# Attention rows in two PSUM banks, scores in 32x32 tiles, and a new order of all calls, in a fused attention and FP4 feed-forward layer

## The chip, the cores and the metric

The kernel runs on one core of one Trainium2 chip. The metric is device time in microseconds, the median of several executions of the whole program.

## What is computed

One layer over 2048 tokens of width 128: retention (linear attention with a decay for each of 8 heads, 16 wide for queries and keys, 32 for values) with an output gate, a residual and a layer norm; then a feed-forward part of width 352 whose operands are all rounded to FP4 in blocks of 16, a residual and a second layer norm. In the reference (cut):

```python
q, k, v = (split_heads(hidden_states @ W) for W in (Wq, Wk, Wv)); q, k = rope(q), rope(k)
scores = jnp.einsum('bhqd,bhkd,hqk->bhqk', q * DQK ** (-0.5), k, decay)
o = jnp.einsum('bhqk,bhkd->bhqd', scores, v)
o = o * jax.lax.rsqrt(jnp.mean(o * o, axis=-1, keepdims=True) + EPS) * g_norm_w
x = layernorm(x + (o.reshape(b, l, VDIM) * silu(hidden_states @ Wg)) @ Wo)
h = silu(fp4_linear(x, w_gate)) * fp4_linear(x, w_up)    # fp4_linear rounds both operands
x = layernorm(x + fp4_linear(h, w_down))
```

## The kernel before

The tokens are 16 chunks `c` of 128, each of two halves `a` of 64. There is no loop over chunks in the program: each engine has one list, written out, of calls such as `scores(5)`, and works through it in order. A call first waits on semaphores for what it reads and, on TensorE (`occupy`, `free`), until the last user of each of its PSUM banks has been read out; then it issues its instructions. So the order of the five lists decides what stands behind what. SyncE's list holds only loads and stores, and ACT's weight loads stand ahead of its list.

One chunk goes through these steps. TensorE projects (`project_qk`, `project_vg`); VectorE multiplies by the rotation tables (`rotate`), POOL adds (`rotate_add`), TensorE transposes (`transpose_qk`) and ACT copies out (`q_even`, `q_odd`, `k_transposed`). `scores` (L330) multiplies keys by queries within each half; VectorE masks them (`mask_scores`, L727). The state `S` of each half comes from `state_product` (L341) and VectorE's `next_state` (L738). The rows of the attention are accumulated in PSUM, transposed (32 features of a head by 64 tokens): `from_state` (L355) starts them with state times query, `values` (L365) adds value times masked score. ACT copies them out (`copy_oT`), `transpose_o` (L372, L373) turns them to tokens by 256 features, ACT squares (`squares`), VectorE gates (`gated`, L748) and sums (`mean_square`), POOL takes the power -1/2 (`rms_rstd`) and multiplies (`gated_output`). Then `transpose_y`, `copy_yT`, `out_projection` (L386 to L388), `ln1_squares`, `ln1_norm`; the rounding of x (`x_amax` to `x_grid_` on VectorE, `x_value` on POOL), `transpose_xq`, `gate` (L421), `up` (L427), `h_product`, the rounding of h likewise (`h_amax`, `h_inv`, `h_ratio_`, `h_plus_`, `h_grid_`, `h_value`), `transpose_h` (L433), `down` (L441), `ln2_sum` and the second norm. At the start VectorE also rounds the two weight tensors (`weights_amax(0)` to `weights_value(1)`); TensorE transposes them (`transpose_gate_up_weights`, `transpose_down_weights`) before it can run `gate(0)`.

All products are in f32. A call of `mm` shows as two weight loads and two matmuls in the trace, a transposition as one of each.

PSUM has 8 banks of 512 f32 columns. Scores of heads 2j and 2j+1 lie in bank j of 0 to 3, one row of tiles for 32 query or key features (row group j of TensorE) by 64 keys. The attention rows of half `a` and heads 4h to 4h+3 lie in bank 2h+a: all four banks 0 to 3. Of the same four, bank 0 also serves `transpose_qk`, bank 1 `transpose_o` (until `gated` has read it), bank 2 `transpose_xq`, bank 3 `transpose_h`. Up to four chunks' buffers exist in SBUF (`c % D`, D = 4), and six of `h_ratio`.

Of the kernel before, what the change touches and what calls it, by code (L numbers as in the profile page):

```python
# [74 lines left out]
def seq_postln_kernel(nc, x, xt, wqk, wvg, wo_g, w_gate_up, w_down, tab, cst, out):  # L75
# [4 lines left out]
    with ExitStack() as ctx:  # L80
# [3 lines left out]
        def sem(name):  # L84
# [76 lines left out]
        BANKS = {"sc": (0, 1, 2, 3), "oT": (0, 1, 2, 3), "o": (1,), "yT": (7,), "qk": (4,), "qkT": (0,),  # L161
                 "vg": (6,), "att": (5,), "xqT": (2,), "gate": (4,), "hT": (3,), "up": (7,),
# [4 lines left out]
        oT_ps = ps[:, 0:4, 0:CH]  # L167
        oT_bank = lambda half, a: ps[:, BANKS["oT"][2 * half + a], 0:CH]
# [12 lines left out]
        wg_T_ps, wu_T_ps = ps[:, 3, 0:I], ps[:, 2, 0:I]  # L181
# [63 lines left out]
        def _(pe_engine):  # L245
# [76 lines left out]
            def scores(c):  # L322
# [22 lines left out]
            def from_state(c):  # L345
# [44 lines left out]
            def transpose_gate_up_weights():  # L390
                pe.wait_ge(c_ident, 1)
                pe.wait_ge(wq_v[0], 1)
                occupy("wgu", (3, 2))
# [50 lines left out]
            warm_up(4); project_qk(0); project_vg(0); transpose_qk(0); project_qk(1); state_product(0); scores(0)  # L444
# [495 lines left out]
```

## Time and profile before

| what | value |
|---|---|
| median of 3 executions | 133.14 us (133.12 to 134.86) |
| the profiled execution | 132.9 us, of which the span from first to last instruction is 131.2 us |
| granted TensorE clock, mean | 0.992 of full speed |
| busy share: TensorE matmuls, VectorE, ACT, POOL | 91%, 84%, 68%, 67% |

Busy time is the union of the instructions' durations. A matmul's duration holds the time in which its results drain, and the next one starts before that; an instruction of VectorE or ACT likewise overlaps the next by about 0.1 us. So a pace is read from one start to the next, not from the durations alone.

### The profile page before, as it was taken

How to read it: one execution, taken by the hardware profiler on the slowest of the kernel's cores; microseconds unless marked ns; L12 is line 12 of the kernel's file. 1: busy time of each engine (PE TensorE's matmuls, PEld its weight loads, DVE VectorE, ACT ScalarE, POOL GpSimd, SP SyncE). 2: the span in 40 equal slices, each digit the busy share in tenths (PEclk: the TensorE clock that was granted, in tenths of full speed). 3: DMA queues.
4: the chain of work that ended last, by engine and by line, in shares of the span. 5: the costliest groups of instructions: out<-in, count | busy, mean ns of one | idle time of the engine just before them, and what ended most of it. 6: DMA issues, size and time to landing. Idle time of an engine off the chain costs nothing.

```text
span 131.2 us, 5084 instructions
## 1 busy us (share of the span) xinstructions
PE 119.2 (91%) x2040; PEld 82.7 (63%) x2040; DVE 110.0 (84%) x329; ACT 88.8 (68%) x311; POOL 87.7 (67%) x124
## 2 busy tenths in 40 slices
PE   4859699989999999999999999899999999999860
PEld 4425257766667676766675576567696788887650
DVE  1249999689589999999999998899999999999810
ACT  3143847557674776839576858778696878898882
POOL 5202726577687849784783869476949797996781
PEclk9999999999999999999999999999999999999996
DMA  3899991000000000000000000000000000011222
GB/s 104 256 273 392 425 440 45 5 5 5 0 5 0 5 0 5 0 7 0 5 2 5 0 5 2 5 0 5 0 5 0 25 2 0 20 40 30 58 80 80
DMA packets 4791, 7.68 MB, mean 59 GB/s; under 512 B 800, under 2 KB 3872, under 8 KB 4512
## 3 DMA queue, kind: packets, MB, share of 16 engines
q1 hardware_dynamic: 3744, 6.60, 14.3%
q10 hardware_dynamic: 1024, 0.76, 1.8%
q8 instruction: 16, 0.26, 0.9%
q14 instruction: 7, 0.06, 0.2%
HBM read 6.31 MB, written 1.05 MB: 56 GB/s over the span
## 4 chain that ended last, share of the span: by engine, by line
PE 66%; DVE 16%; DMA 6%; issue 4%; ACT 3%; POOL 2%; SPq 1%; POOLq 0%; DVEq 0%
PE ps L313 7%; PE ps L441 7%; DMA tabs_sb<-rope_tables 6%; PE ps L421 6%; PE ps L427 6%; PE ps L330 5%; PE ps L307 4%; PE ps L355 4%; PE ps L365 4%; DVE probs L727 3%; PE ps L433 3%; PE ps L386 3%; PE ps L341 3%; PE ps L388 2%; PE ps L387 2%
## 5 line engine op out<-in xcount | busy, mean ns | idle before, releaser
L859 POOL TENSOR_TENSOR rstd_h<-ms,minus_half 128x8 f32<-128x8 f32 x16 | 26.8, 1672 | 6.9 <-DVE ms L743 6.8
L313 PE MATMUL ps<-w_vg,xT_sb 128*128 128x512 f32 x32 | 17.4, 625 | 1.5 <-DVE S L738 1.1
L854 POOL TENSOR_TENSOR qk<-rope 128x256 f32<-128x256 f32 x16 | 11.7, 729 | 9.7 <-DVE rope L721 9.7
L878 POOL TENSOR_TENSOR xq<-x_ratio,xs 128x128 f32<-128x128 f32 x16 | 7.8, 489 | 11.9 <-DVE x_ratio L656 11.9
L441 PE MATMUL ps<-wd_T,hT 128*128 128x128 f32 x96 | 14.1, 283 | 1.3 <-DVE r L757 0.7
L721 DVE TENSOR_TENSOR rope<-ps,tabs_sb 128x512 f32<-128x512 f32 x16 | 11.0, 687 | 4.6 <-DMA tabs_sb<-rope_tables 3.3
L870 POOL TENSOR_TENSOR rstd<-veps,minus_half 128x1 f32<-128x1 f32 x16 | 9.3, 579 | 7.7 <-DVE veps L752 7.7
L886 POOL TENSOR_TENSOR hq<-h_ratio,hs 128x352 f32<-128x352 f32 x16 | 13.0, 815 | 1.7 <-DVE h_ratio L656 1.4
L441 PEld LDWEIGHTS ps<-wd_T,hT 128*128 128x128 f32 x96 | 12.1, 191 | 3.1 <-ACT hT L483 1.5
L727 DVE TENSOR_TENSOR probs<-ps,causal 128x512 f32<-128x512 f32 x16 | 11.0, 690 | 2.8 <-PE ps L330 2.4
L421 PE MATMUL ps<-wgu_T,xqT 128*128 128x352 f32 x32 | 13.3, 496 | 0.0
L483 ACT ACTIVATE oT<-ps 128x256 f32<-128x256 f32 x16 | 6.1, 382 | 9.9 <-PE ps L365 9.8
L427 PE MATMUL ps<-wgu_T,xqT 128*128 128x352 f32 x32 | 12.2, 464 | 0.0
L307 PE MATMUL ps<-w_qk,xT_sb 128*128 128x256 f32 x32 | 10.8, 421 | 1.0 <-DMA xT_sb<-x_transposed 1.0
L864 POOL TENSOR_TENSOR y<-gate_o,rstd_h 128x256 f32<-128x256 f32 x16 | 10.4, 651 | 0.5
L484 ACT ACTIVATE q_eo<-ps,consts 128x128 f32<-128x128 f32 x32 | 10.7, 376 | 0.0
L738 DVE SCALAR_TENSOR_TENSOR S<-S,consts,ps 128x64 f32<-128x64 f32 x31 | 8.3, 269 | 2.6 <-PE ps L341 2.2
L874 POOL TENSOR_TENSOR rstd<-veps,minus_half 128x1 f32<-128x1 f32 x16 | 9.1, 579 | 1.5 <-ACT r_sq L580 1.5
L483 ACT ACTIVATE v_sb<-ps 128x256 f32<-128x256 f32 x16 | 6.3, 391 | 5.0 <-PE ps L313 5.0
L561 ACT ACTIVATE silu_h<-ps 128x352 f32<-128x352 f32 x16 | 7.4, 463 | 2.8 <-PE ps L421 2.5
L501 ACT ACTIVATE h_magic<-h_ratio 128x352 bf16<-128x352 f32 x16 | 7.9, 496 | 1.5 <-DVE h_ratio L647 1.4
L483 ACT ACTIVATE hT<-ps 128x384 f32<-128x384 f32 x16 | 7.8, 487 | 1.6 <-PE ps L433 1.6
(110 smaller groups left out, 340.1 us busy)
## 6 DMA issues: line engine op xcount, KB each, us to landing
tabs_sb<-rope_tables SPq DMA_DIRECT2D x1, 2048.0 KB, 12.0
tabs_sb<-rope_tables SPq DMA_DIRECT2D x1, 1280.0 KB, 8.1
out<-x SPq DMA_DIRECT2D x16, 64.0 KB, 1.5
tabs_sb<-rope_tables SPq DMA_DIRECT2D x1, 512.0 KB, 4.6
xT_sb<-x_transposed SPq DMA_DIRECT2D x1, 512.0 KB, 7.6
xT_sb<-x_transposed SPq DMA_DIRECT2D x1, 320.0 KB, 5.5
tabs_sb<-rope_tables SPq DMA_DIRECT2D x1, 256.0 KB, 3.6
w_vg<-in_w_vg ACTq DMA_DIRECT2D x1, 256.0 KB, 3.9
```

The costliest lines, as they stand in the source:

```text
L307: mm(qk_ps, xT(c), w_qk[:], start=True, stop=True).then_inc(qk_pe, 1)
L313: mm(vg_ps, xT(c), w_vg[:], start=True, stop=True).then_inc(vg_pe, 1)
L421: mm(gate_ps, xqT[:, c % D, :], wgu_T[:, 0:I], start=True, stop=True).then_inc(gate_pe, 1)
L427: mm(up_ps, xqT[:, c % D, :], wgu_T[:, I:2 * I], start=True, stop=True).then_inc(up_pe, 1)
L441: last = mm(down_ps, hT[:, c % D, t, :], wd_T[:, t, :], start=t == 0, stop=t == 2)
L483: copy = lambda o, i: nc.scalar.activation(o, i, ACT.Copy)
L484: scaled = lambda o, i, by: nc.scalar.activation(o, i, ACT.Identity, scale=by)
L721: vec.tensor_tensor(rope[:, c % D, :, :], qk_ps.unsqueeze(1).to_broadcast([128, 2, 256]), tabs(c).rearrange("p (t n) -> p t n", t=2), ALU. ...
L727: vec.tensor_tensor(probs[:, c % D, :, :].rearrange("p (j e) q -> p j e q", e=2), all_sc_ps.rearrange("p j (e q) -> p j e q", e=2), causal ...
L854: gp.tensor_tensor(g16(qk[:, c % D, :]), g16(rope[:, c % D, 0, :]), g16(rope[:, c % D, 1, :])[:, :, ::-1, :], ALU.add).then_inc(qk_p, 1)
L859: gp.tensor_tensor(rstd_h[:, c, :], ms[:, c, :], minus_half[:], ALU.pow).then_inc(rms_p, 1)
L886: gp.tensor_tensor(hq[:, c % D, 0:I].rearrange("p (n k) -> p n k", k=BLK), h_ratio[:, c % 6, :].rearrange("p (n k) -> p n k", k=BLK), hs[: ...
```

## The change

- The attention rows lie in two banks: half `a` in bank 1+a, with the even heads in columns 0 to 63 and the odd in 64 to 127 (`oT_ps(a)`). Heads 2j and 2j+1 stand in the 32 partitions of slot `(j + 2a) % 4`: in the second half the upper and lower 64 partitions are swapped. `from_state` and `values` run over e (even, odd) outside.
- `copy_oT` becomes three ACT instructions: the first half whole (128 partitions by 128), the second half in two pieces of 64 partitions by 128 that undo the swap.
- `transpose_o` thus gives the features in the order (e, j, d); `squares` and `gated` read PSUM through views that put them back. `o` moves to bank 2, `xqT` to bank 1, the transposed weights to banks 1 and 3.
- `scores` runs over four groups of 32 keys in place of two of 64: 16 calls of `mm` for 8.
- `h_ratio_(c)` waits for POOL's `h_value(c - 6)`, the last reader of its buffer.
- The lists of TensorE, ACT, VectorE and POOL are ordered anew. The sets of calls are the same, SyncE's list and all DMAs are as before.

```diff
-        BANKS = {"sc": (0, 1, 2, 3), "oT": (0, 1, 2, 3), "o": (1,), "yT": (7,), "qk": (4,), "qkT": (0,),
-                 "vg": (6,), "att": (5,), "xqT": (2,), "gate": (4,), "hT": (3,), "up": (7,),
+        BANKS = {"sc": (0, 1, 2, 3), "oT": (1, 2), "o": (2,), "yT": (7,), "qk": (4,), "qkT": (0,),
+                 "vg": (6,), "att": (5,), "xqT": (1,), "gate": (4,), "hT": (3,), "up": (7,),
...
-        oT_ps = ps[:, 0:4, 0:CH]
-        oT_bank = lambda half, a: ps[:, BANKS["oT"][2 * half + a], 0:CH]
+        oT_ps = lambda a: ps[:, BANKS["oT"][a], 0:C].rearrange("p (e q) -> p e q", q=CH)
+        oT_slot = lambda j, a: 32 * ((j + 2 * a) % NP)
...
-                for a in range(2):
+                for k in range(4):
                     for j in range(NP):
-                        rows, keys = slice(32 * j, 32 * j + 32), slice(CH * a, CH * a + CH)
+                        rows, keys = slice(32 * j, 32 * j + 32), slice(32 * k, 32 * k + 32)
                         last = mm(sc_ps(j)[keys, :], kT[rows, c % D, keys],
-                                  q_eo[rows, c % D, a, :, :].rearrange("p e q -> p (e q)"), start=True, stop=True)
+                                  q_eo[rows, c % D, k // 2, :, :].rearrange("p e q -> p (e q)"), start=True, stop=True)
...
-                for a in range(2):
-                    for n in range(NH):
-                        j, e, slot32 = n // 2, n % 2, n % 4
-                        rows = slice(32 * j, 32 * j + 32)
-                        mm(oT_bank(n // 4, a)[32 * slot32:32 * slot32 + 32, :], S[rows, (2 * c + a) % 8, e * DV:(e + 1) * DV],
-                           q_eo[rows, c % D, a, e, :], start=True, stop=False)
+                for e in range(2):
+                    for a in range(2):
+                        for j in range(NP):
+                            rows, slot = slice(32 * j, 32 * j + 32), oT_slot(j, a)
+                            mm(oT_ps(a)[slot:slot + 32, e, :], S[rows, (2 * c + a) % 8, e * DV:(e + 1) * DV],
+                               q_eo[rows, c % D, a, e, :], start=e == 0, stop=False)
...
-                for n in range(NH):
-                    slot32 = n % 4
-                    for a in range(2):
-                        keys = slice(CH * a, CH * a + CH)
-                        last = mm(oT_bank(n // 4, a)[32 * slot32:32 * slot32 + 32, :],
-                                  v_sb[keys, c % D, n * DV:(n + 1) * DV], probs[keys, c % D, n, :], start=False, stop=True)
+                for e in range(2):
+                    for j in range(NP):
+                        for a in range(2):
+                            n, keys, slot = 2 * j + e, slice(CH * a, CH * a + CH), oT_slot(j, a)
+                            last = mm(oT_ps(a)[slot:slot + 32, e, :], v_sb[keys, c % D, n * DV:(n + 1) * DV],
+                                      probs[keys, c % D, n, :], start=False, stop=e == 1)
...
-                copy(oT[:, c % D, :, :, :].rearrange("p h a q -> p (h a) q"), oT_ps).then_inc(oT_act, 1)
+                copy(oT[:, c % D, :, 0, :], oT_ps(0))
+                copy(oT[0:64, c % D, :, 1, :], oT_ps(1)[64:128])
+                copy(oT[64:128, c % D, :, 1, :], oT_ps(1)[0:64]).then_inc(oT_act, 1)
...
-                nc.scalar.activation(o_sq[:, c % D, :, 0:DV], o_ps.rearrange("p (h d) -> p h d", d=DV), ACT.Square,
+                nc.scalar.activation(o_sq[:, c % D, :, 0:DV].rearrange("p (j e) d -> p j e d", e=2),
+                                     o_ps.rearrange("p (e j d) -> p j e d", e=2, d=DV), ACT.Square,
...
-                vec.tensor_tensor(gate_o[:, c % D, :], o_ps, silu_g[:, c % D, :], ALU.mult).then_inc(gate_v, 1)
+                vec.tensor_tensor(jed(gate_o[:, c % D, :]), o_ps.rearrange("p (e j d) -> p j e d", e=2, d=DV),
+                                  jed(silu_g[:, c % D, :]), ALU.mult).then_inc(gate_v, 1)
...
-            def h_ratio_(c): quant_ratio(h(c), sh(c), blocks(h_ratio[:, c % 6, :]), hquant_v, c)
+            def h_ratio_(c):
+                if c >= 6:
+                    dve.wait_ge(hq_p, c - 5)
+                quant_ratio(h(c), sh(c), blocks(h_ratio[:, c % 6, :]), hquant_v, c)
```

The lists, as far as the text below speaks of them. TensorE, the start and two later places:

```diff
-            warm_up(4); project_qk(0); project_vg(0); transpose_qk(0); project_qk(1); state_product(0); scores(0)
-            project_vg(1); from_state(0); values(0); state_product(1); project_qk(2); transpose_qk(1); transpose_o(0)
...
-            transpose_o(1); transpose_qk(2); transpose_gate_up_weights(); state_product(2); transpose_down_weights()
...
-            state_product(3); values(2); project_qk(5); transpose_o(2); transpose_qk(3); out_projection(1)
-            state_product(4); scores(3); project_qk(6); from_state(3); values(3); project_qk(7); transpose_qk(4)
-            transpose_o(3); transpose_y(2); transpose_xq(0); project_vg(5); gate(0); scores(4); out_projection(2)
...
-            from_state(4); state_product(5); values(4); project_qk(8); transpose_o(4); transpose_qk(5); transpose_y(3)
-            project_vg(6); transpose_xq(1); up(0); scores(5); out_projection(3); from_state(5); state_product(6)
-            values(5); gate(1); transpose_o(5); transpose_qk(6); transpose_y(4); project_vg(7); project_qk(9)
-            transpose_xq(2); up(1); scores(6); out_projection(4); from_state(6); state_product(7); values(6); gate(2)
+            warm_up(4); project_qk(0); project_vg(0); transpose_qk(0); state_product(0); scores(0); project_qk(1)
+            project_vg(1); from_state(0); values(0); state_product(1); transpose_qk(1); project_qk(2); transpose_o(0)
...
+            project_qk(4); transpose_y(0); transpose_o(1); transpose_gate_up_weights(); transpose_down_weights()
...
+            state_product(3); transpose_qk(3); project_qk(5); transpose_o(2); out_projection(1); state_product(4)
+            scores(3); project_qk(6); from_state(3); values(3); transpose_qk(4); project_qk(7); transpose_y(2)
+            transpose_o(3); transpose_xq(0); project_vg(5); scores(4); gate(0); out_projection(2); from_state(4)
...
+            transpose_xq(1); up(0); scores(5); out_projection(3); gate(1); from_state(5); state_product(6); values(5)
+            transpose_qk(6); project_qk(9); transpose_y(4); transpose_o(5); project_vg(7); transpose_xq(2); up(1)
+            scores(6); out_projection(4); from_state(6); state_product(7); values(6); gate(2); transpose_qk(7)
```

ACT, VectorE and POOL, the start:

```diff
-            copy_v(0); silu_g_(0); q_even(0); q_odd(0); k_transposed(0); silu_g_(1); copy_v(1); copy_oT(0); squares(0)
+            silu_g_(0); k_transposed(0); copy_v(0); q_odd(0); q_even(0); weights_magic(0); copy_v(1); silu_g_(1)
+            copy_oT(0); k_transposed(1); squares(0); q_odd(1); q_even(1); copy_v(2); silu_g_(2); weights_magic(1)
...
-            rotate(0); weights_amax(0); next_state(0, 0); next_state(0, 1); rotate(1); mask_scores(0); weights_inv(0)
-            weights_amax(1); weights_ratio(0); next_state(1, 0); rotate(2); next_state(1, 1); mean_square(0)
-            weights_inv(1); gated(0); weights_ratio(1); weights_plus(0); mask_scores(1); weights_grid(0)
+            rotate(0); weights_amax(0); weights_inv(0); next_state(0, 0); weights_ratio(0); next_state(0, 1)
+            rotate(1); mask_scores(0); scale_wo(); weights_plus(0); weights_amax(1); next_state(1, 0); weights_inv(1)
+            next_state(1, 1); rotate(2); gated(0); mean_square(0); weights_ratio(1); mask_scores(1); weights_grid(0)
...
-            rotate_add(5); rms_rstd(3); gated_output(3); ln1_rstd(2); x_value(1); rotate_add(6); rms_rstd(4)
+            rotate_add(5); rotate_add(6); rms_rstd(3); rotate_add(7); gated_output(3); ln1_rstd(2); x_value(1)
```

## Rows read from the trace of the kernel before

**Rows 1.** The page, part 1: busy time, share of the span, instructions of each engine.

```profile
PE 119.2 (91%) x2040; PEld 82.7 (63%) x2040; DVE 110.0 (84%) x329; ACT 88.8 (68%) x311; POOL 87.7 (67%) x124
```

**Rows 2.** The page, part 4: shares of the chain that ended last.

```profile
PE 66%; DVE 16%; DMA 6%; issue 4%; ACT 3%; POOL 2%; SPq 1%; POOLq 0%; DVEq 0%
```

**Rows 3.** Table by stretch: busy time of each engine (instructions), then granted clock, DMA.

```profile
10.00:20.00 10.00, 8.57 (x184) 4.74 (x185) 9.93 (x24) 5.73 (x17) 3.78 (x4) 1.00 1.02 413
20.00:40.00 20.00, 19.55 (x430) 13.20 (x428) 16.25 (x47) 12.95 (x47) 14.37 (x18) 1.00 0.02 7
40.00:100.00 60.00, 59.09 (x1175) 40.44 (x1153) 57.03 (x178) 42.94 (x154) 43.43 (x56) 1.00 0.01 3
100.00:125.00 25.00, 23.85 (x219) 19.10 (x218) 23.24 (x70) 20.90 (x77) 20.88 (x31) 1.00 0.08 23
```

**Rows 4.** Timeline of TensorE, 44 to 51 us: start, length, instruction, count.

```profile
44.39 0.47 PE L330 MATMUL ps<-q_eo,kT 32*64 32x128 f32 x16
...
46.76 0.86 PE L421 MATMUL ps<-wgu_T,xqT 128*128 128x352 f32 x2
47.45 0.27 PE L372 MATMUL ps<-ident,oT 128*128 128x128 f32 x1
...
48.11 1.02 PE L313 MATMUL ps<-w_vg,xT_sb 128*128 128x512 f32 x2
48.97 0.59 PE L307 MATMUL ps<-w_qk,xT_sb 128*128 128x256 f32 x2
...
50.20 0.63 PE L330 MATMUL ps<-q_eo,kT 32*64 32x128 f32 x16
```

**Rows 5.** Timeline of VectorE, 4 to 24 us; in brackets idle time and its end.

```profile
9.24 0.60 DVE L738 SCALAR_TENSOR_TENSOR S<-S,consts,ps 128x64 f32<-128x64 f32 x2 [1.48 <-PE ps L341]
...
11.05 0.33 DVE L673 TENSOR_SCALAR wr_small<-wr_small 128x44 f32<-128x44 f32 x1
...
11.80 0.51 DVE L639 TENSOR_REDUCE wr_small<-wd_nat 128x22 f32<-128x352 f32 x1
12.22 0.88 DVE L647 SCALAR_TENSOR_TENSOR wr_ratio<-wgu_nat,wr_small 128x704 f32<-128x704 f32 x1
...
16.56 0.68 DVE L727 TENSOR_TENSOR probs<-ps,causal 128x512 f32<-128x512 f32 x1
```

**Rows 6.** Timeline of TensorE, 5 to 33 us: two blocks.

```profile
8.05 0.70 PE L307 MATMUL ps<-w_qk,xT_sb 128*128 128x256 f32 x2 [1.01 <-DMA xT_sb<-x_transposed]
...
24.54 0.45 PE L355 MATMUL ps<-q_eo,S 32*32 32x64 f32 x32
```

**Rows 7.** Groups of instructions: count, busy us, mean ns; idle time before them.

```profile
L483 ACT ACTIVATE oT<-ps 128x256 f32<-128x256 f32 x16 | 6.1, 382 | 9.9 <-PE ps L365 9.8
...
L483 ACT ACTIVATE xqT<-ps 128x128 f32<-128x128 f32 x16 | 4.5, 280 | 1.4 <-PE ps L415 1.2
...
L727 DVE TENSOR_TENSOR probs<-ps,causal 128x512 f32<-128x512 f32 x16 | 11.0, 690 | 2.8 <-PE ps L330 2.4
```

**Rows 8.** Waits: who for whom, total us, times, longest.

```profile
PEld ps L372 <- ACT oT L483: 2.9, 10, 0.4
...
PEld ps L330 <- ACT q_eo L484: 3.5, 6, 1.2
```

**Rows 9.** Timeline of TensorE, 5 to 33 us: the same block twice.

```profile
11.96 0.44 PE L341 MATMUL ps<-v_sb,qk 64*32 64x64 f32 x16
...
20.62 0.34 PE L341 MATMUL ps<-v_sb,qk 64*32 64x64 f32 x16
```

**Rows 10.** Timeline, 26 to 33 us: transposed rows and their gating, chunk 3.

```profile
30.91 0.27 PE L372 MATMUL ps<-ident,oT 128*128 128x128 f32 x1
...
32.20 0.37 DVE L748 TENSOR_TENSOR gate_o<-ps,silu_g 128x256 f32<-128x256 f32 x1
```

**Rows 11.** Timeline, 96 to 110 us: POOL's `h_value(6)` and VectorE's `h_ratio_(12)`.

```profile
103.01 0.89 POOL L886 TENSOR_TENSOR hq<-h_ratio,hs 128x352 f32<-128x352 f32 x1 [0.38 <-PE ps L433]
...
109.01 0.52 DVE L647 SCALAR_TENSOR_TENSOR h_ratio<-h_blocks,hs 128x352 f32<-128x352 f32 x1
```

More of the change, by code:

```diff
@@ L458, in _ @@
-            transpose_qk(8); transpose_y(6); project_vg(9); project_qk(11); transpose_xq(4); up(3); scores(8)
-            out_projection(6); from_state(8); state_product(9); values(8); gate(4); transpose_qk(9); transpose_o(8)
-            transpose_y(7); project_vg(10); project_qk(12); transpose_xq(5); up(4); scores(9); out_projection(7)
-            from_state(9); state_product(10); values(9); gate(5); transpose_o(9); transpose_qk(10); transpose_y(8)
-            project_vg(11); project_qk(13); up(5); transpose_xq(6); out_projection(8); scores(10); gate(6)
@@ L463, in _ @@
-            from_state(10); state_product(11); values(10); project_qk(14); transpose_o(10); transpose_qk(11)
-            project_vg(12); transpose_xq(7); transpose_y(9); scores(11); up(6); out_projection(9); from_state(11)
-            state_product(12); values(11); gate(7); transpose_qk(12); transpose_o(11); transpose_y(10); project_vg(13)
-            project_qk(15); up(7); transpose_xq(8); out_projection(10); scores(12); gate(8); from_state(12)
-            values(12); state_product(13); transpose_o(12); transpose_qk(13); transpose_y(11); project_vg(14)
@@ new lines, in _ @@
+            transpose_xq(1); up(0); scores(5); out_projection(3); gate(1); from_state(5); state_product(6); values(5)
+            transpose_qk(6); project_qk(9); transpose_y(4); transpose_o(5); project_vg(7); transpose_xq(2); up(1)
+            scores(6); out_projection(4); from_state(6); state_product(7); values(6); gate(2); transpose_qk(7)
+            transpose_o(6); transpose_y(5); project_vg(8); project_qk(10); transpose_xq(3); up(2); scores(7)
+            out_projection(5); from_state(7); state_product(8); values(7); gate(3); transpose_qk(8); transpose_o(7)
@@ new lines, in _ @@
+            transpose_y(6); project_vg(9); project_qk(11); transpose_xq(4); up(3); scores(8); out_projection(6)
+            gate(4); from_state(8); state_product(9); values(8); transpose_qk(9); project_qk(12); transpose_y(7)
+            transpose_o(8); project_vg(10); transpose_xq(5); up(4); scores(9); out_projection(7); from_state(9)
+            state_product(10); values(9); transpose_qk(10); gate(5); transpose_o(9); transpose_y(8); project_vg(11)
+            project_qk(13); transpose_xq(6); out_projection(8); scores(10); gate(6); up(5); from_state(10); values(10)
@@ new lines, in _ @@
+            state_product(11); transpose_qk(11); project_qk(14); transpose_o(10); transpose_y(9); project_vg(12)
+            transpose_xq(7); out_projection(9); scores(11); up(6); from_state(11); values(11); state_product(12)
+            transpose_qk(12); gate(7); transpose_o(11); transpose_y(10); project_vg(13); project_qk(15)
+            transpose_xq(8); up(7); scores(12); out_projection(10); from_state(12); state_product(13); values(12)
+            gate(8); transpose_qk(13); transpose_o(12); transpose_y(11); project_vg(14); up(8); transpose_xq(9)
@@ new lines, in _ @@
+            out_projection(11); scores(13); gate(9); from_state(13); state_product(14); values(13); transpose_qk(14)
+            transpose_h(0); transpose_y(12); transpose_o(13); project_vg(15); up(9); transpose_xq(10)
+            out_projection(12); scores(14); gate(10); from_state(14); state_product(15); values(14); transpose_y(13)
+            transpose_qk(15); transpose_o(14); transpose_h(1); up(10); out_projection(13); transpose_xq(11); down(0)
+            scores(15); gate(11); up(11); from_state(15); values(15); transpose_y(14); transpose_h(2); down(1)
@@ L829, in _ @@
+            h_grid_(13); h_plus_(14); ln2_sum(10); h_grid_(14); h_product(15); h_amax(15); ln2_sum(11); h_inv(15)
+            h_ratio_(15); ln2_sum(12); h_plus_(15); h_grid_(15); ln2_sum(13); ln2_sum(14); ln2_sum(15)
         @block.gpsimd
```

203 lines of the change are left out of this document (97 added, 106 removed).

## Prediction

> **What bounds the kernel now.** I read the busy shares first: TensorE 91%, VectorE 84%, ACT 68%, POOL 67% [rows 1]. Two engines are nearly full, so the next view is the chain that ended last: 66% of the span on TensorE and 16% on VectorE [rows 2]. Then the table by stretch tells where VectorE idles: 0.07 us between 10 and 20 us, 3.75 us between 20 and 40, 2.97 us between 40 and 100, 1.76 us between 100 and 125 [rows 3]. That is 8.5 us in 115, and since the change takes no work from VectorE, no order gains more than this and what lies ahead of 10 us. Last the timelines. From one `scores` to the next (44.39 to 50.20 us) TensorE has 5.81 us of work end to end: the six transpositions from 47.45 to 48.11 follow each other at 0.11 us, `project_vg` takes 0.86 [rows 4]. In the middle, then, TensorE sets the pace with VectorE just behind; in the start (10 to 20 us) it is VectorE, with the rounding of the weights; at the end the backlog of h on VectorE.
>
> The profiled execution took 132.9 us: a span of 131.2 and 1.7 around it. I make the sum against 132.9 and add 0.2 us at the end, by which the median of 133.14 lies above it.
>
> **The start: -1.2 us.** VectorE idles 1.48 us until 9.24 us, waiting for `state_product(0)` [rows 5]. That call stands on TensorE behind `project_qk(1)`, which itself waited 1.01 us for a transfer of xT [rows 6]. The new lists put `state_product(0)` and `scores(0)` ahead of `project_qk(1)`, and on VectorE `weights_inv(0)` (11.05 to 11.80, so 0.75 us) and `weights_ratio(0)` (0.88 us) [rows 5] into the time in which it idles. These 1.6 us leave the full stretch after 10 us; `scale_wo` (about 0.3 us, an estimate between those two sizes of neighbours) enters it. So `mask_scores(1)`, now at 16.56 us [rows 5], should start near 15.3, and `from_state(2)`, now at 24.54 [rows 6], some 1.2 us earlier. Because VectorE was full there, and has a backlog until the end, this gain should live to the end. Bounds: -1.5 (the whole gap) and 0 (if TensorE then stands at `transpose_gate_up_weights`, which still waits for the last steps of rounding, and loses it again).
>
> **Scores in 32x32 tiles: +0.6 us.** Each chunk issues 16 pairs of weight load and matmul more. A block of 16 pairs of 64 columns takes 0.34 us [rows 9], one of 32 pairs of 64 columns 0.45 [rows 6]: 7 ns a pair, because the pairs lie on different tiles of the array and run side by side. `scores` is a block of 16 pairs now, of 0.47 us [rows 4]; each tile runs its two passes one after the other, before as after. Eight more tiles shift the second passes by at most 8 x 7 ns = 0.06 us. I take 0.04 us, 16 times, on TensorE's path. Low end: -0.02 us each, since the block of 32 in 32x32 tiles takes 0.02 less than `scores` now; -0.3 in all. High end: the same 16 pairs took 0.44 us in place of 0.34 where they came right behind another block of small matmuls [rows 9], 7 ns a pair more; 31 such steps are 0.21, with the shift 0.27 us a chunk and 4.3 us in all. I take the value near the low end because before most `scores` stands a large matmul, beside which the pairs can be fetched.
>
> The Trainium skill (TensorE: Matmul & The Clock Gate, section "Wait — 56ns, not 53.3ns?") states that from one matmul's start to the next never less than about 25 ns pass, however small they are. By it 16 more pairs would cost 0.4 us a chunk and 6.4 us in all, for 138.5 us. The trace disagrees: at 25 ns the 32 pairs of [rows 6] would need 0.78 us for their starts alone, and the block is over in 0.45.
>
> **Three copies in place of one: no time of its own.** The 256-column copy takes 382 ns, a 128-column one 280 [rows 7]. Instructions of ACT overlap by about 0.1 us, so three take 2 x 0.18 + 0.28 = 0.64 us: the rows are ready 0.26 us later, and ACT works 16 x 0.26 = 4.2 us more, from 68% to 71% of the span. Bounds: 0.1 us if the two half-height pieces ran in one piece's time, 0.46 us with no overlap. The cover is the next item's; where it is gone, each chunk pays 0.26 us, 4.2 us in all.
>
> **Waits for the copied rows: -0.6 us.** `transpose_o` waits 2.9 us for `copy_oT` in ten places [rows 8]. That is counted on the weight loads, mostly beside a running `gate`: `transpose_o` starts 0.69 us after `gate` [rows 4], whose two passes, by columns against `project_vg`, need 0.86 x 352/512 = 0.59. So a wait costs TensorE about 0.1 us. Bank 0 no longer holds attention rows, so `transpose_qk(c+1)`, and often `project_qk` and `transpose_y`, move between `values(c)` and `transpose_o(c)`: 0.22 to 0.87 us of work, more than the 0.26 us by which the copies end later. I take six places at 0.1 us. Bounds: -2.9 and 0.
>
> **Queries ready earlier: -0.4 us.** The weight loads of `scores` wait 3.5 us for ACT's `q_eo` in six places [rows 8], and the block at 50.20 us takes 0.63 in place of 0.47 us [rows 4]. With `transpose_qk` earlier and ACT's `k_transposed` and `q_even` right behind the copies, I take two or three places at 0.16 us. Bounds: -3.5 and 0.
>
> **A shorter way round bank 2: +0.6 us.** `scores(c+1)` needs the bank of `o`, so it waits for `gated(c)`. In chunk 3 `transpose_o` starts at 30.91 and `gated` ends at 32.57: 1.66 us [rows 10]. The new list leaves between `transpose_o(3)` and `scores(4)` only `transpose_xq(0)` and `project_vg(5)`: 0.22 + 0.11 + 0.86 = 1.19 us [rows 4], so TensorE stands up to 0.47 us; `gate(0)` and `transpose_y(2)` have moved elsewhere, and behind the waiting `scores` all of TensorE's list queues, with ACT's `silu_of_gate(0)` waiting for that. Chunk 2 is alike, with less. Where `up` or `gate` stays in between (chunks 5 to 13) the cover is 1.9 us or more. I take 0.4 + 0.2. Bounds: 0, and 0.47 in thirteen chunks, 6.1.
>
> **Edits without a price.** `squares` and `gated` read PSUM through a view of four dimensions, with as many elements. `mask_scores` reads such a view at 690 ns for 512 elements [rows 7], 1.35 ns each; `gated` now takes 0.37 us for 256 [rows 10], 1.45 each. So I take nothing, with 0 to 0.1 us a chunk, 1.6 us, as bounds. The new wait in `h_ratio_(c)` would hold up all of VectorE's list, and POOL's `h_value(c)` behind it. But `h_value(c-6)` is long done: in the closest case POOL ends `h_value(6)` at 103.90 and `h_ratio_(12)` starts at 109.01 [rows 11]. Only if the new lists ate 5 us would it cost anything. POOL's calls change places with one another and POOL has a third of its time free [rows 1]; a `rotate_add` that comes late would hold `transpose_qk`, but these move ahead, not back. No DMA moves.
>
> **Sum.** -1.2 + 0.6 - 0.6 - 0.4 + 0.6 = -1.0 us: 131.9 against the profiled 132.9, and 132.1 on the median's scale.
>
> **The rivals.** *The new order closes the gaps between 20 and 40 us.* VectorE idles 3.75 us there [rows 3], and with attention a little ahead x and h have work for it sooner. If half of it goes, with the start, the copied rows and the queries as above and `scores` at +0.6: -1.2 - 1.9 - 0.6 - 0.4 + 0.6 = -3.5, so 129.6. For it: VectorE has much more work later that could move there. Against it: TensorE is busy 19.55 of these 20 us. Chance 0.23.
>
> *Scores become bound by the issue of small matmuls.* Their block then runs at the pace of [rows 9] behind another block: +4.3 in place of +0.6 us, 135.8 in all. It decides from the point where fewer than the block's pairs stand ready when it may start, as when it stands behind a wait. Chance 0.08. The Trainium skill's rule above (TensorE: Matmul & The Clock Gate, "Wait — 56ns, not 53.3ns?") would make it worse, at 138.5 us; I give it 0.01 of that 0.08, since the rows speak against it.
>
> *Bank 2 holds up every chunk.* With ACT's longer copies the way from `transpose_o` to `gated` grows past its cover everywhere: 0.47 us in thirteen chunks, +6.1 in place of +0.6: 137.6. Chance 0.04.
>
> *The change does not free what it says.* Banks 1 and 2 are two of the four that `scores` fills, so `from_state` still waits for `mask_scores`; the gain at the start is lost at the weights. Then only `scores` costs: 0 to +0.6, 133.4. Chance 0.15.
>
> **How the numbers follow.** The forecast keeps 0.50, with 130.6 to 133.8 as its own range. A time is told from no change here at about 2%, which is below 130.5 and above 135.8. Faster: 0.21 of the first rival and 0.04 of the forecast's lower edge, 0.25. Slower: half of the issue-bound case, the bank case and 0.03 for a stall that I don't see, 0.11. The rest, 0.64, is within. The range from 129.3 to 135.2 leaves out about 0.1 on each side.
>
> **What would show it.** Right: `mask_scores(1)` before 15.6 us and no idle time of 1.5 us on VectorE ahead of 9.3; the block of L330, then 32 pairs, at 0.47 to 0.55 us; three copies of about 280 ns, ending 0.6 to 0.7 us after the first starts; the wait of L372 for the copied rows well under 2.9 us; a wait of L330 for `gated` of 0.3 to 0.5 us in chunk 4. Wrong: a block of L330 of 0.7 us or more; waits for `gated` in most chunks; VectorE idle under 2 us between 20 and 40; or `from_state(2)` still near 24.5.

## The result, and the profile after

The changed kernel took 141.15 us (140.19 to 143.40), the kernel before 134.69 beside it: 1.056 times as long (95% interval 1.052 to 1.061). Some executions of a kernel fall in a slower state, so ratios here and below compare the others alone and need not be the quotient of the medians. Forecast were 132.1 us, with a range to 135.2. In the first profiled execution (143.4 us) the granted clock fell near 83 us, so the same kernel was profiled again, and this second trace, which has no such fall, is read here: 141.27 us, a span of 139.5 and 1.8 around it.

> The changed kernel once more, nothing altered, for a second trace of it. The clock fell once in its first profile, near 83 us, and chunks 11 to 13 stretched there by 3 to 5 us. If these stalls belong to the lists (theory A), they stand here too, at a clock of 1.00, and scores(15) starts near 107. If they came from the fall of the clock (theory B), scores(15) starts near 103 to 104, the other chunks stay at 6.2 to 6.4 us, and the kernel is at 140 to 141 us only if something else was lost.

By its main sign theory A: the long chunks 11 and 12 are there at a clock of 1.00. `scores(15)` starts at 105.34 us (98.97 before), between the numbers of the two theories. Busy shares and chain, to set beside [rows 1, 2]:

```profile
PE 124.6 (89%) x2296; PEld 83.0 (59%) x2296; DVE 113.6 (81%) x329; ACT 96.3 (69%) x343; POOL 90.1 (65%) x124
PE 59%; DVE 23%; issue 6%; ACT 5%; DMA 3%; POOL 1%; POOLq 0%; ACTq 0%; DVEq 0%
```

TensorE has 256 pairs of weight load and matmul more, and its share fell; "issue", time in which an engine waits for nothing that the profile shows, went from 4% to 6% of the chain. The table by stretch, beside [rows 3]:

```profile
10.00:20.00 10.00, 9.74 (x196) 5.02 (x197) 9.07 (x21) 5.45 (x16) 4.19 (x4) 1.00 1.02 405
20.00:40.00 20.00, 18.92 (x430) 12.56 (x428) 15.81 (x43) 14.48 (x54) 13.21 (x17) 1.00 0.03 11
40.00:100.00 60.00, 56.71 (x1238) 36.10 (x1236) 53.28 (x162) 43.27 (x159) 40.97 (x50) 1.00 0.01 3
```

Between 40 and 100 us TensorE is idle 3.3 us (0.9 before) and VectorE 6.7 (3.0). By the starts of `scores`, the 8.3 us of span came so: 1.4 until `scores(2)` (23.17 against 21.76), 2.1 until `scores(11)`, 2.4 in chunks 11 and 12, 0.4 until `scores(15)`, 2.0 from there to the end of the span (34.2 us against 32.2). Waits, timelines of ACT and of TensorE:

```profile
PEld ps L330 <- ACT q_eo L484: 4.0, 6, 1.0
PEld ps L372 <- ACT oT L483: 2.7, 10, 0.5
...
49.23 0.84 ACT L483 ACTIVATE oT<-ps 128x128 f32<-128x128 f32 x3 [0.35 <-PE ps L365]
...
50.13 0.33 PE L372 MATMUL ps<-ident,oT 128*128 128x128 f32 x1
...
77.63 0.50 PE L330 MATMUL ps<-q_eo,kT 32*32 32x128 f32 x32
```

Neither wait of [rows 8] has shrunk by much (3.5 and 2.9 us before). The three copies take 0.84 us (forecast 0.64), and `transpose_o` starts 0.06 us behind their end. A block of `scores` mostly takes 0.50 to 0.51 us, within the forecast.

### The profile page after: what moved, and what is told of

It is laid out like the page before. It is cut to its first block, busy times and chain, and to the rows that moved or that the text cites. A ratio compares the mean times of both kernels' runs of the same rounds, so it can differ in the third digit from the quotient of the medians.

```text
span 141.6 us, 5644 instructions
## 1 busy us (share of the span) xinstructions
PE 126.2 (89%) x2296; PEld 84.0 (59%) x2296; DVE 113.5 (80%) x329; ACT 96.3 (68%) x343; POOL 89.9 (63%) x124
## 4 chain that ended last, share of the span: by engine, by line
PE 59%; DVE 22%; issue 6%; ACT 5%; DMA 3%; POOL 1%; POOLq 0%; ACTq 0%; DVEq 0%
PE ps L313 10%; PE ps L330 6%; PE ps L421 5%; PE ps L307 4%; PE ps L427 4%; DVE probs L730 4%; PE ps L355 4%; PE ps L365 4%; PE ps L441 3%; PE ps L341 3%; DMA w_vg<-in_w_vg 3%; DVE h_ratio L655 2%; PE ps L386 2%; DVE hs L642 2%; DVE h_blocks L781 2%
## 5 line engine op out<-in xcount | busy, mean ns | idle before, releaser
L313 PE MATMUL ps<-w_vg,xT_sb 128*128 128x512 f32 x32 | 19.1, 684 | 0.7 <-DMA w_vg<-in_w_vg 0.7
L483 ACT ACTIVATE oT<-ps 64x128 f32<-64x128 f32 (+1 forms) x48 | 13.1, 272 | 9.7 <-PE ps L365 9.3
L886 POOL TENSOR_TENSOR xq<-x_ratio,xs 128x128 f32<-128x128 f32 x16 | 8.3, 520 | 11.8 <-DVE x_ratio L659 11.8
L872 POOL TENSOR_TENSOR y<-gate_o,rstd_h 128x256 f32<-128x256 f32 x16 | 11.2, 698 | 0.9
L650 DVE SCALAR_TENSOR_TENSOR h_ratio<-h_blocks,hs 128x352 f32<-128x352 f32 x16 | 9.7, 603 | 0.3
L365 PE MATMUL ps<-probs,v_sb 64*32 64x64 f32 x512 | 8.9, 226 | 1.1 <-issue 1.1
L355 PEld LDWEIGHTS ps<-q_eo,S 32*32 32x32 f32 x512 | 5.0, 107 | 8.2 <-DVE probs L730 5.8
```

What stands on the lines that cost most here:

```text
L313: mm(vg_ps, xT(c), w_vg[:], start=True, stop=True).then_inc(vg_pe, 1)
L365: last = mm(oT_ps(a)[slot:slot + 32, e, :], v_sb[keys, c % D, n * DV:(n + 1) * DV], probs[keys, c % D, n, :], start=False, stop=e == 1)
L483: copy = lambda o, i: nc.scalar.activation(o, i, ACT.Copy)
L872: gp.tensor_tensor(y[:, c % D, :].rearrange("p (h d) -> p h d", d=DV), gate_o[:, c % D, :].rearrange("p (h d) -> p h d", d=DV), rstd_h[:, ...
```

## Experiments: layout and lists crossed

First theories: A, the new lists cost the time; B, the new layout (copies and tiles) does; C, only both together.

> Layout, 32x32 scores and three copies of the change, with all four lists of calls as before. Theory A (the lists cost the time: project_qk(1) behind scores(0) holds up rotate(1) and mask_scores(0), and transpose_o meets rows that are not there): 133.5 to 135.5 us, a loss of 0 to 2. Theory B (the layout costs it: copies that end 0.46 us later and scores 0.1 us longer in each of 16 chunks, some 0.55 us a chunk): 139 to 142 us. Theory C (they only cost together): 134 to 137 us here, and little in the crossed kernel too.

Against the changed kernel:

```diff
-            warm_up(4); project_qk(0); project_vg(0); transpose_qk(0); state_product(0); scores(0); project_qk(1)
+            warm_up(4); project_qk(0); project_vg(0); transpose_qk(0); project_qk(1); state_product(0); scores(0)
...
```

(and so on, all four lists.)

It took 1.051 times the kernel before (1.045 to 1.057), 140.14 us: theory B. The waits show where:

```profile
PEld ps L372 <- ACT oT L483: 8.7, 15, 0.9
```

> The lists of calls of the change (with the wait that h_ratio needs under them) on the old layout: four banks, one copy, 64-key scores. Theory A (the lists cost the time): 139 to 141 us, mask_scores(0) near 11.9 us as in the changed kernel. Theory B (the layout costs it): 132.5 to 135 us. Theory C (they only cost together): 134 to 136 us.

Against the kernel before:

```diff
-            warm_up(4); project_qk(0); project_vg(0); transpose_qk(0); project_qk(1); state_product(0); scores(0)
+            warm_up(4); project_qk(0); project_vg(0); transpose_qk(0); state_product(0); scores(0); project_qk(1)
...
+                if c >= 6:
+                    dve.wait_ge(hq_p, c - 5)
```

1.039 (1.029 to 1.049), 139.05 us: nearest to theory A. So each half costs, and they don't add up: lists and layout were fitted to each other. On the old banks the lists' early `transpose_qk(c+1)` needs bank 0, which still holds attention rows (its transpositions wait for `copy_oT` in this trace), so this run overstates the lists. They were therefore tried on their own banks, without the two costs of the layout:

> The two banks and swapped quadrants of the change with all lists of calls, the 64-key scores and one copy as before; it leaves out the swap back, so the second half of the tokens gets the heads in another order. The kernel with all of the layout and the old lists took 140.1 us, 6.6 above the kernel before; 32x32 scores alone cost 1.8 of it. Theory L (three copies are the rest): 133.5 to 135 us here. Theory B (the banks are the rest, by scores that wait for gated in bank 2): 137 to 139 us.

> The changed kernel with 64-key scores and one copy: its lists of calls and its banks, without the two costs. It leaves out the swap back, so the second half of the tokens gets the heads in another order. The same kernel with the old lists took 133.7 us. Theory A (the new lists are slower by themselves, at the start and by waits): with the sums of the single edits, 141.2 - 3.6 - 1.2 = 136.4 us. Theory L (the lists are good and were only spoilt by late rows and more pairs): 132 to 134 us.

Both are the changed kernel with this edit and that of `scores64` below, the first with the old lists:

```diff
-                copy(oT[:, c % D, :, 0, :], oT_ps(0))
-                copy(oT[0:64, c % D, :, 1, :], oT_ps(1)[64:128])
-                copy(oT[64:128, c % D, :, 1, :], oT_ps(1)[0:64]).then_inc(oT_act, 1)
+                copy(oT[:, c % D, :, :, :].rearrange("p h a q -> p a h q"),
+                     ps[:, 1:3, 0:C].rearrange("p a (e q) -> p a e q", q=CH)).then_inc(oT_act, 1)
```

The banks and the quadrants cost nothing: 1.002 (0.997 to 1.008). The new lists alone cost 1.015 (1.013 to 1.018), 135.17 us. So the loss has three parts: copies, tiles, and a rest in the lists.

## Experiments: the copies

> The kernel before with its one copy of attention rows cut in three (128 columns of 128 rows, and twice 128 columns of 64 rows), nothing else. Theory L (the copies end 0.46 us later and transpose_o, next in the old list, waits for them in each of 16 chunks): 137.5 to 138.5 us, the 4.6 us that scores and banks leave of the 6.6 of the whole layout. The forecast's term: 0 where other work covers it, 4.2 us where none does, with ACT's instructions overlapping, so 133.5 to 137.8. If the three copies only cost together with the banks: 133.5 us.

```diff
-                copy(oT[:, c % D, :, :, :].rearrange("p h a q -> p (h a) q"), oT_ps).then_inc(oT_act, 1)
+                copy(oT[:, c % D, :, 0, :], ps[:, 0:4:2, 0:CH])
+                copy(oT[0:64, c % D, :, 1, :], ps[0:64, 1:4:2, 0:CH])
+                copy(oT[64:128, c % D, :, 1, :], ps[64:128, 1:4:2, 0:CH]).then_inc(oT_act, 1)
```

1.035 (1.027 to 1.043), 137.76 us, some 4.5 us for a term that the forecast put at 0. The waits and the copies of one chunk:

```profile
PEld ps L372 <- ACT oT L483: 6.5, 11, 0.7
...
48.59 0.72 ACT L483 ACTIVATE oT<-ps 128x128 f32<-128x128 f32 x3 [0.73 <-PE ps L365]
```

> The changed kernel with one copy of 256 columns in place of the three. It leaves out the swap back, so the second half of the tokens gets the heads in another order; nothing else of the work changes. Theory L (late rows: three copies end 0.84 us after the first starts, one after about 0.38, and under the new lists most of these 0.46 us are paid, since transpose_o waits for them): 16 chunks at 0.2 to 0.4 us, 135 to 138 us. Theory O (the lists themselves, by the start and by chunks 11 to 13, cost the time): 139.5 to 141 us.

The edit is the diff of one copy above, alone. 1.040 (1.031 to 1.049) against 1.056 with three: 2.2 us by the ratios, 1.2 by the medians (139.94). O is nearer than L: the new lists cover half or more of what the copies cost on the old ones.

## Experiments: the tiles and the fetch of instructions

> The kernel before with scores alone in 32x32 tiles, 32 pairs a chunk. The forecast's term: +0.04 us a chunk, 133.5 to 134.5 us. If the pairs become bound by their issue: +0.27 a chunk, 137 us or more. If the block is hidden beside the wait for mask_scores or beside large matmuls: no difference.

1.014 (1.004 to 1.023), 135.90 us: 1.8 us, between the forecast's term and the issue-bound case. The block is not issue-bound: from its first to its last start pass 0.23 to 0.25 us in most chunks (0.21 before). But `mask_scores` starts 0.69 us after the block's start in place of 0.58 (medians). One of each, in the kernel before (for the block at 44.39 us of [rows 4]) and in the changed one (for the block at 77.63 us above):

```profile
44.97 0.69 DVE L727 TENSOR_TENSOR probs<-ps,causal 128x512 f32<-128x512 f32 x1
```

```profile
78.32 0.69 DVE L730 TENSOR_TENSOR probs<-ps,causal 128x512 f32<-128x512 f32 x1 [0.21 <-PE ps L330]
```

And TensorE stands once in the middle of a block of `values`, with nothing to wait for:

```profile
90.37 0.40 PE L365 MATMUL ps<-probs,v_sb 64*32 64x64 f32 x18
91.55 0.34 PE L365 MATMUL ps<-probs,v_sb 64*32 64x64 f32 x14 [0.79 <-issue]
```

The changed kernel has two such stands, in `state_product(12)` and `values(12)` (timeline of TensorE, then the DMA view from 85 to 89 us, 0.1 us a slice):

```profile
81.16 0.30 PE L341 MATMUL ps<-v_sb,qk 64*32 64x64 f32 x2 [0.74 <-issue]
...
86.78 0.51 PE L365 MATMUL ps<-probs,v_sb 64*32 64x64 f32 x22
88.38 0.32 PE L365 MATMUL ps<-probs,v_sb 64*32 64x64 f32 x10 [1.10 <-issue]
...
DMA  0000000070000000000000000000000000000000
...
q8 instruction: 1, 0.02, 1.8%
```

One packet of 0.02 MB of instructions starts at 85.8 us and takes 1.8% of 16 engines' 4 us, 1.15 us; TensorE goes on at 88.38, 1.4 us after its end. In all eighteen stands of this kind of 0.4 us or more, in nine traces, it goes on 1.2 to 1.6 us after a packet's end. Two of them, of 0.4 us, lie in `values(1)`, in `old_layout_new_order` and in `order_tail` (below), which have no 32x32 tiles: the tiles add stands, but a list without them can have one too. The page of the profile counts 18 such packets in the changed kernel and 16 in the one before, for 4592 and 4080 records of matmuls and weight loads. In records, the stands are at 3200 and 3451, and at 3705 in the kernel above: steps of about 251.

> The changed kernel with scores back in tiles of 64 keys: 16 pairs a chunk less, 512 instructions less on TensorE. Theory F (TensorE outruns the fetch of its instructions: in two traces of the changed kernel it stands 0.9 and 1.3 us in the middle of blocks of small matmuls at pairs 3200 and 3451 of its records, waiting for no semaphore, 1.4 us after the end of a transfer of 16 KB of instructions; 512 instructions less are two such transfers less): these two stalls go or move, and with 0.1 us a chunk of shorter scores the kernel gains 2.5 to 4 us, 137 to 138.7 us. Theory S (the forecast's term for the tiles, 0.04 us a chunk, and no more): 140 to 141 us.

```diff
-                for k in range(4):
+                for a in range(2):
                     for j in range(NP):
-                        rows, keys = slice(32 * j, 32 * j + 32), slice(32 * k, 32 * k + 32)
+                        rows, keys = slice(32 * j, 32 * j + 32), slice(CH * a, CH * a + CH)
...
```

1.024 (1.017 to 1.031), 137.56 us, and no stand in its trace: undoing the tiles gives back 3.2 points of 5.6, 3.6 us by the medians and 4.3 by the ratios. Theory F. Two further runs tell the stands from the tiles and from the calls in which they fell:

> The changed kernel with 64-key scores in chunks 0 to 3 alone: 128 instructions of TensorE less ahead of pair 3200, so that its blocks of 256 instructions begin elsewhere in the chunk. Theory F (TensorE stood in blocks of small matmuls because the next block of instructions had not come): the stands of 0.9 and 1.3 us at state_product(12) and values(12) go or move to other places; if they go, 138.3 to 139.3 us, if they move to other dense places, 140 to 140.7. Theory S (they belong to these calls and their buffers): both stay at state_product(12) and values(12), and four chunks gain 0.1 us each, 140.6 to 140.9.

```diff
-                for k in range(4):
+                n = 2 if c < 4 else 4
+                for k in range(n):
                     for j in range(NP):
-                        rows, keys = slice(32 * j, 32 * j + 32), slice(32 * k, 32 * k + 32)
+                        rows, keys = slice(32 * j, 32 * j + 32), slice(C // n * k, C // n * (k + 1))
...
```

128 instructions less moved the stands to `values(5)`, `values(6)` and `state_product(8)` (records 1440, 1691 and 1942, the same step), 2.9 us idle in all:

```profile
43.92 0.42 PE L366 MATMUL ps<-probs,v_sb 64*32 64x64 f32 x22 [0.80 <-issue]
```

Its four times were 137.22, 142.63, 143.26 and 143.72 us, without an interval: neither theory's number, but the places moved as F says. The 6.5 us between its times stay open: only a run at the upper end was profiled.

> The changed kernel with nine more dummy matmuls of 128 columns on TensorE before 8.6 us: two more ahead of project_qk(0), three behind it, four behind transpose_qk(0), in time in which it waits for w_vg and for the copy of v. Theory K (the start was lost because TensorE ran its matmuls at half pace until 13.3 us: project_vg(1) took 1.06 us a pass there, 0.59 in the kernel before, and what stood ahead was idle time): the passes come down to 0.59 us by about 9 us, mask_scores(0) starts at 10.5 to 11.0 in place of 11.7, and 0.8 to 1.5 us are gained, 139.7 to 140.4. Theory W (the start is set by the weights' rounding on VectorE or by rotate(1)): no gain, 141 us.

```diff
-            warm_up(4); project_qk(0); project_vg(0); transpose_qk(0); state_product(0); scores(0); ...
+            warm_up(6); project_qk(0); warm_up(3); project_vg(0); transpose_qk(0); warm_up(4); state_product(0); scores(0); ...
```

1.088 (1.081 to 1.095), 144.49 us, against both theories, and the best witness for F: nine dummy matmuls with their weight loads are 36 records more (18 matmuls and 18 loads; the expectation of `scores64_warm` says 18 in all), so other calls lie on the edges, and TensorE now stands four times from `values(9)` to `values(12)` (at 69.00, 76.31, 83.09 and 90.50 us), 4.2 us of idle time where the changed kernel has 1.8:

```profile
69.00 0.30 PE L365 MATMUL ps<-probs,v_sb 64*32 64x64 f32 x4 [1.29 <-issue]
```

The Trainium skill (Runtime: NRT & Kernel Launch, section "Instruction fetch mechanics") says that instructions come in blocks of 256, fetched while the block before runs, and that the cost of crossing an edge is mostly hidden. The block size agrees with the steps of about 251 records; hidden the cost is not at these edges, which fall into runs of small matmuls.

## Experiments: the start

> The changed kernel with project_qk(1) back ahead of state_product(0) on TensorE. Theory R (the start was lost because VectorE's rotate(1) waits for project_qk(1), and mask_scores(0) stands behind it in VectorE's list): mask_scores(0) starts at 10.5 to 11.0 us in place of 11.9, from_state(2) near 24.7 in place of 25.7, and the kernel gains 0.8 to 1.3 us, 140.0 us. Theory W (the rounding of the weights sets the start anyway): mask_scores(0) is earlier, from_state(2) stays within 0.3 us, and the time stays at 141.

```diff
-            ... transpose_qk(0); state_product(0); scores(0); project_qk(1)
+            ... transpose_qk(0); project_qk(1); state_product(0); scores(0)
```

1.053 (1.044 to 1.063): no clear gain, and `mask_scores(0)` at 12.14 us (11.73 in the changed kernel), so theory R's earlier start did not come (nor did theory W's). In this trace TensorE's half pace, told of below, lasted longest of all, to 15.8 us, so the swap by itself at full pace is not shown. In the changed kernel VectorE did wait 0.57 us for `project_qk(1)`:

```profile
11.12 0.69 DVE L724 TENSOR_TENSOR rope<-ps,tabs_sb 128x512 f32<-128x512 f32 x1 [0.57 <-PE ps L307]
```

but what made it late was TensorE's pace. `project_vg(1)` in the changed kernel, and with the dummy matmuls:

```profile
10.80 1.92 PE L313 MATMUL ps<-w_vg,xT_sb 128*128 128x512 f32 x2
```

```profile
10.45 1.12 PE L313 MATMUL ps<-w_vg,xT_sb 128*128 128x512 f32 x2 [0.26 <-DVE S L741]
```

The first has two passes of 1.06 us (0.59 at full pace): 1.2 GHz in place of 2.4, though the granted clock in the table reads 1.00: the trace has a record of the clock only from 13.3 us on, where the passes become short (from 6.2 us on in the kernel before), and the table's mean leaves out what lies ahead. Half pace lasts until 13 to 16 us in the traces with the new lists and no dummy matmuls; with the old lists it ends between 5 and 10 us. Ahead of the rise the changed kernel's TensorE stood 0.80 us until 8.60, for the copy of v. With dummy matmuls in these waits the full pace comes at 5 to 7 us, with the first or second pass of `project_vg(0)`, in all six kernels that have them, and in `warm_after` `mask_scores(0)` came at 10.92 us. The Trainium skill (TensorE: Matmul & The Clock Gate, section "What's actually happening") calls half pace the default that activity releases; the runs agree.

> The changed kernel with 64-key scores (137.6 us) and the nine dummy matmuls in TensorE's early waits. In the kernel with 32x32 scores they brought the full pace of TensorE forward from 13.3 to 6.5 us and mask_scores(0) from 11.7 to 10.9, but the kernel lost 3 us. Theory F (it lost them to four stands in blocks of small matmuls, 0.4 to 1.3 us each, because 18 instructions more move the edges of the fetched blocks; with 512 instructions less there are none): the early start is kept to the end, 136.0 to 137.2 us. Rival (dummy matmuls cost something by themselves, later on): 138 to 140 us.

1.017 (1.009 to 1.025), 136.12 us, 1.4 less than `scores64`, no stand: theory F and the start.

> The kernel before with the nine dummy matmuls in TensorE's early waits. Its traces with the old lists came to the full pace between 6 and 10 us; where that was late, mask_scores(0) came 0.3 to 0.6 us later. Theory K (the early pace is worth its time): 132.3 to 133.1 us, the best of all. Rival (the edges of the instruction blocks move here too, and TensorE stands in small matmuls): 134 to 136 us.

0.994 (0.990 to 0.997), 133.06 us, with ten times between 132.75 and 133.30 where the kernel before had 133.20 to 136.02 beside it. It is the one version that beats both kernels, and steadier. How long TensorE stays at half pace differed from trace to trace; that this is what spreads the times of the kernel before is not shown.

## Experiments: the end

From `scores(15)` to the last compute instruction (2 us ahead of the span's end) pass 32.2 to 32.3 us with the new lists, whatever the layout, and 30.1 to 30.4 with the old. VectorE takes h and x first: `gated(15)` comes 7.3 us after `scores(15)` (4.9 before), in `order_alone` at 106.53 after 99.27. There:

```profile
103.91 1.09 DVE L649 SCALAR_TENSOR_TENSOR h_ratio<-h_blocks,hs 128x352 f32<-128x352 f32 x1
```

> The kernel with the new lists, 64-key scores and one copy (135.2 us; it leaves out the swap back, so the second half of the tokens gets the heads in another order), with chunk 15 moved ahead in three lists: transpose_o(15) ahead of transpose_h(2) and down(1) on TensorE, squares(15) ahead of copy_hT(2) on ACT, mean_square(15) and gated(15) ahead of h_ratio_(11) on VectorE. Theory E (the new lists are slow at the end: from scores(15) to the end 32.2 us pass, 30.1 with the old lists, because gated(15) comes 7.3 us after scores(15) in place of 4.9): gated(15) at 5.0 to 5.8 us after scores(15), the end 1 to 2 us sooner, 133.2 to 134.2 us. Rival: the end is set by the sum of VectorE's work on h, and a call moved ahead gives nothing: 135.0 to 135.3.

```diff
-            h_ratio_(11); ln2_sum(1); mean_square(15); h_grid_(9); h_plus_(11); x_amax(13); gated(15); x_inv(13)
+            mean_square(15); gated(15); h_ratio_(11); ln2_sum(1); h_grid_(9); h_plus_(11); x_amax(13); x_inv(13)
...
-            ... transpose_y(14); transpose_h(2); down(1); transpose_o(15); transpose_h(3); ...
+            ... transpose_y(14); transpose_o(15); transpose_h(2); down(1); transpose_h(3); ...
...
-            copy_yT(14); copy_hT(2); squares(15); ...
+            copy_yT(14); squares(15); copy_hT(2); ...
```

`gated(15)` came at 4.7 us after `scores(15)`, and the end still at 32.1: theory E falls. The time was 1.010 (1.005 to 1.014), 135.34 us.

> The new lists on their banks with 64-key scores and one copy (it leaves out the swap back, so the second half of the tokens gets the heads in another order), chunk 15 ahead as in order_tail, and the dummy matmuls at the start. If the start and the end are all that the new lists cost, this is at the kernel before or a little below it: 132.3 to 133.7 us. If something else in the lists costs time, above 134 us.

0.999 (0.995 to 1.003), 133.65 us. Its trace beside `warm_before`, which has the same start: `from_state(2)` at 24.14 us against 25.11; from `scores(1)` to `scores(15)` 82.65 against 82.98; to the end 32.08 against 30.25. The new lists gain 0.9 up to `scores(1)` and 0.3 in the middle, and lose 1.8 at the end.

> The mended kernel of the new lists (64-key scores, one copy, dummy matmuls at the start; it leaves out the swap back, so the second half of the tokens gets the heads in another order), with the calls that stand behind scores(15), copy_oT(14), mask_scores(15) and gated_output(14) in the order of the kernel before. In order_tail and order_mended the time from scores(15) to the end stayed at 32.1 us although gated(15) came 2.6 us sooner. Theory T (the rest of the end's order sets it: h_product(13) to (15) come 0.8, 1.5 and 2.6 us later than with the old lists): 30.2 to 30.6 us from scores(15) to the end, 131.6 to 132.3 us. Rival (the state in which the new lists reach scores(15) sets it): 31.8 to 32.2 us to the end, 133.3 to 133.8.

1.002 (0.999 to 1.006), 133.93 us. The end came 31.24 us after `scores(15)`, between the two theories, but `scores(15)` itself came 1.1 us late: from `scores(14)` on, 38.3 us against 38.1 in `order_mended` and 36.3 in `warm_before`. In the old order ACT's `magic_h(9)` stands ahead of `copy_yT(13)`. Here it waits for VectorE's `h_ratio_(9)`, and TensorE's `up(10)`, ahead of `scores(15)`, for that copy:

```profile
95.90 0.50 ACT L501 ACTIVATE h_magic<-h_ratio 128x352 bf16<-128x352 f32 x1 [0.82 <-DVE h_ratio L649]
...
96.72 0.86 PE L427 MATMUL ps<-wgu_T,xqT 128*128 128x352 f32 x2 [0.88 <-ACT yT L483]
```

`h_ratio_(9)` starts 3.4 us after `scores(14)` in `order_alone`, `order_mended` and `old_end`, and 2.3 in the kernel before and in `warm_before`. So the state in which the lists arrive counts: VectorE is behind with h, and the old order of the end does not suit that. What else the 1.8 us consist of stays open. After `scores(14)` VectorE's instructions, each against the shortest of its form, are 1.6 us longer in sum in `order_alone` than in `banks_old_order`, as the 1.09 us above (0.51 mostly), which lies beside a POOL instruction on h. But in `old_end` they are only 0.3 us longer, VectorE idles 5.4 us there in place of 4.1, and the end is as late; so their length alone is not the cause. That was read, not tried.

> The same kernel with no quadrant swapped at all: both halves of the tokens in the same quadrants, so that one copy serves and nothing is left out; from_state then works on four tiles of the array in place of eight. If tiles that come twice as often cost nothing (from_state's 32 pairs are no longer bound by their passes), it takes the time of old_end, 131.6 to 132.3 us. If from_state goes through its four tiles one after the other (its block 0.1 to 0.2 us longer in 16 chunks), 133.2 to 135.5 us.

```diff
-        oT_slot = lambda j, a: 32 * ((j + 2 * a) % NP)
+        oT_slot = lambda j, a: 32 * j
```

1.018 (1.013 to 1.022), 135.93 us: `from_state`'s block takes 0.58 us to the next call's start, 0.39 with the swap. The swap is worth 2 us here, and its three copies cost 1.2 to 2.2 of it again (`one_copy`).

## Why the prediction was wrong

By its own terms, with what the runs showed in their place. The steps that failed are the pace taken for the start, the cover of the copies, the term for the tiles, and the end, which has no term:

- **Start, -1.2:** lost instead; `mask_scores(1)` at 17.02 us (forecast 15.3). The mechanism was right: with TensorE at full pace the new lists bring `mask_scores(1)` to 15.91 (17.14 in `warm_before`) and `from_state(2)` 0.97 us earlier. The step that failed is that TensorE's calls keep the durations of the trace of before, which had come to full pace at 6.2 us; in the changed kernel it came at 13.3 us.
- **Scores, +0.6:** the block was sized right (0.43 to 0.44 us to the next call, 0.40 to 0.41 before), the term was not: about 4 us in the changed kernel. 1.8 us are two stands at edges of fetched instructions, which the trace of before does not have and which 512 more instructions brought; `mask_scores` starts 0.1 us later in each chunk, 1.6 us if every chunk pays it. What is left of the 4 us is not split up. Neither the rival of issue-bound pairs nor its block of 0.7 us was seen.
- **Three copies, 0:** the step that failed is the cover: 4.5 us were paid on the old lists, 1.2 to 2.2 on the new. That 4.5 lies near the named price without cover, 4.2, is luck: the rows there came 0.34 us later (0.72 for 0.38), 5.4 us in 16 chunks, not 0.26. In the changed kernel they came 0.46 us later, because the overlap that I assumed isn't there: 0.84 us, my upper bound.
- **Waits for copied rows, -0.6:** no gain, 2.7 us in ten places (2.9 before). The calls moved ahead of `transpose_o` covered the longer copies only to the point where it starts 0.06 us behind them.
- **Queries, -0.4:** no gain, 4.0 us in six places (3.5 before).
- **Bank 2, +0.6:** did not come. `scores` waits for `gated` for 0.3 us in all, and for 0.6 in the kernel before, where `o` lay in bank 1; with the old lists the banks cost nothing (1.002).
- **Without a price:** right: `gated` 417 ns in the mean (409 before), no wait for the h buffers seen.
- **Not in the sum:** the end, +2.0 us. I read VectorE's backlog at the end and didn't follow the new list through it; VectorE is 1.1 us further behind with h there (`h_ratio_(9)`), and the rest stays open.

The first rival asked that idle time between 20 and 40 us go; VectorE's rose from 3.75 to 4.2 us. Of the prediction's sums one is off: the 138.5 us add 6.4 us for `scores` to a sum that already holds them at 0.6; in its place they make 137.9.

## What to carry to other kernels

Count an edit's instructions, not only their time: here TensorE's came by transfer, and 512 more, or 36 that moved the rest along, put it at a stand in its densest blocks; such a stand shows as "issue" inside a block. A price "if the cover is gone" belongs into the sum until a row shows the cover. Where the first microseconds decide, look whether TensorE is at full pace in them; dummy matmuls in its waits made a kernel 0.6% faster and steadier.

## Unexpected of the hardware

- TensorE at a stand for instructions goes on 1.2 to 1.6 us after the end of a 16 KB packet of them (eighteen stands, nine traces).
- Not all copies on ACT overlap: a 64-row copy that stays in its quadrants starts 0.10 us before the end of the copy of all rows ahead of it (`old_copies3`); one that swaps quadrants (`again`), or follows a copy of the other half, starts 0.01 us behind it. Three take 0.72 us unswapped and 0.84 swapped.
- TensorE's half pace at the start does not show in the granted clock of the table, which reads 1.00 while passes take 1.06 us in place of 0.59; the trace's record of the clock starts with the rise.
